# Routed tiles of a mixture-of-experts layer: turned in squares of 32 on VectorE instead of whole on TensorE

## The reference

```python
def _layernorm(x, axis=-1, eps=1e-05):
    m = jnp.mean(x, axis=axis, keepdims=True)
    v = jnp.var(x, axis=axis, keepdims=True)
    return (x - m) / jnp.sqrt(v + eps)

def _swiglu(x, w1, w2, w3):
    return jax.nn.silu(x @ w1) * (x @ w3) @ w2

# _L0_ffn_ref: D = 512, F = 352, E = 8, TOPK = 2
y = _swiglu(xf, sw1, sw2, sw3)                       # shared part
scores = jax.nn.softmax(xf @ gate_w, axis=-1)
weights, indices = jax.lax.top_k(scores, TOPK)
cw = jnp.zeros((N, E)).at[jnp.arange(N)[:, None], indices].add(weights)
for e in range(E):
    h = _swiglu(xf, rw1[e], rw2[e], rw3[e])
    y = y + cw[:, e:e + 1] * h

# reference
x = x + 0.5 * _L0_ffn_ref(_layernorm(x), ...)
x = x + _L0_attn_ref(_layernorm(x), ...)
x = x + 0.5 * _L0_ffn_ref(_layernorm(x), ...)
```

## Time and profile before

| | |
|---|---|
| runs | 1639.86 us median of 3 (1637.92 to 1640.12) |
| profiled execution | 1637.68 us, span 1635.9 us |
| PE busy | 1566.0 us, 96% of the span, 8356 instructions |
| DVE busy | 868.2 us, 53% |
| ACT busy | 657.3 us, 40% |
| POOL busy | 894.9 us, 55% |
| chain that ended last | PE 71%, DMA 9%, DVE 7% |
| tile stages, first to last write of a tile's output | 197.5 to 1579.3 us, the attention between them |

### The profile page before, as it was taken

The page is one execution under the profiler, slowest core; times in us unless marked ns, Lnnn a source line. Parts: engine busy times, 40 slices in busy tenths (PEclk is TensorE's granted clock), DMA queues, the critical chain, the costliest instruction groups (busy, mean ns, idle before and its releaser), DMA issues.

```text
span 1635.9 us, 24109 instructions
## 1 busy us (share of the span) xinstructions
PE 1566.0 (96%) x8356; PEld 1140.7 (70%) x8356; DVE 868.2 (53%) x1482; ACT 657.3 (40%) x974; POOL 894.9 (55%) x745
## 2 busy tenths in 40 slices
PE   6999999999998898999999999999999999999996
PEld 5777899999986674444444444337778898899985
DVE  4554322222267686777777777667554422222226
ACT  4421322232232315666666666763431222222321
POOL 3206385503756947787887878510405277333635
PEclk9999999999999999999999999999999999999998
DMA  9306454423363321212112121124105265333338
GB/s 338 136 1 229 180 187 168 152 78 133 119 214 121 84 66 45 40 30 45 34 36 44 31 36 23 25 51 134 58 1 187 93 232 183 127 132 133 133 91 256
DMA packets 89344, 180.15 MB, mean 110 GB/s; under 512 B 30224, under 2 KB 31120, under 8 KB 86928
## 3 DMA queue, kind: packets, MB, share of 16 engines
q1 hardware_dynamic: 76400, 104.95, 21.4%
q0 software_dynamic: 12832, 73.67, 12.7%
HBM read 106.48 MB, written 55.97 MB: 99 GB/s over the span
## 4 chain that ended last, share of the span: by engine, by line
PE 71%; DMA 9%; DVE 7%; ACT 3%; SPq 3%; issue 3%; POOL 3%; POOLq 0%; DVEq 0%; ACTq 0%
PE PS L1190 9%; PE PS L1192 9%; PE PS L1191 9%; PE PS L1423 7%; PE PS L1437 6%; PE PS L1404 6%; DMA xn<-x_routed 4%; PE PS L1453 3%; DMA xs<-x_routed 2%; PE PS L1327 2%; PE PS L1332 2%; PE PS L1330 2%; PE PS L1329 2%; PE PS L1331 2%; PE PS L1328 2%
## 5 line engine op out<-in xcount | busy, mean ns | idle before, releaser
L1676 ACT ACTIVATE PT<-PS 128x1024 f32<-128x1024 f32 x256 | 258.2, 1025 | 124.3 <-PE PS L1423 122.9
L1973 DVE TENSOR_REDUCE nmf_later<-PS 128x1 f32<-128x1024 f32 x160 | 194.1, 1219 | 58.2 <-PE PS L1404 57.7
L1437 PE MATMUL PS<-PT,V 128*32 128x512 f32 x1024 | 202.5, 604 | 0.0
L2041 POOL TENSOR_TENSOR W<-raw,W 128x544 fp32r<-128x544 f32 x144 | 190.0, 1353 | 1.5
L1423 PE MATMUL PS<-QS,KS 98*128 98x512 f32 x512 | 177.2, 430 | 3.7 <-DVE nmf_first L1973 2.0
L982 POOL TENSOR_TENSOR added<-PT 128x1024 f32<-128x1024 f32 x56 | 136.2, 2433 | 75.4 <-ACT PT L1676 75.4
L1423 PEld LDWEIGHTS PS<-QS,KS 98*128 98x128 f32 x512 | 84.8, 189 | 128.2 <-issue 50.7
L1404 PE MATMUL PS<-KS,QS 96*128 96x512 f32 x512 | 168.5, 411 | 5.1 <-ACT PT L1676 2.3
L1940 DVE TENSOR_TENSOR thid<-thid,PS 128x352 f32<-128x352 f32 x78 | 40.7, 521 | 245.7 <-ACT thid L1607 245.7
L2029 POOL DMA_DIRECT2D raw<-ffn_w x18 | 10.0, 554 | 248.6 <-POOLq L2027 192.3
L1190 PE MATMUL PS<-xh,W 128*128 128x512 f32 x352 | 141.7, 403 | 4.1 <-DVE xl L1703 1.6
(11 more groups left out here) (200 smaller groups left out, 3832.9 us busy)
## 6 DMA issues: line engine op xcount, KB each, us to landing
raw<-ffn_w POOLq DMA_DIRECT2D x18, 2176.0 KB, 10.4
y_routed<-ytile SPq DMA_DIRECT2D x78, 256.0 KB, 2.0
xn<-x_routed SPq DMA_DIRECT2D x40, 256.0 KB, 3.2
x_routed<-xq SPq DMA_DIRECT2D x1, 9984.0 KB, 29.4
xs<-x_routed SPq DMA_DIRECT2D x38, 256.0 KB, 3.8
QS<-later_hi SPq DMA_DIRECT2D x112, 64.0 KB, 2.0
raw<-ffn_w SPq DMA_DIRECT2D x6, 768.0 KB, 6.0
raw<-ffn_w SPq DMA_DIRECT2D x16, 272.0 KB, 4.2
```

Source lines behind the costliest of these rows:

```text
L1437: e.matmul(PS[i * QUARTER:(i + 1) * QUARTER, ob, :], V[:, b * QT + kt, g, :], PT[:, u % PTBUF, kt % 2 * GRP:(kt % 2 + 1) * GRP], start=rou ...
L1676: e.activation(PT[:, u % PTBUF, :], PS[:, i:i + 2, :].rearrange("p b n -> p (b n)"), ACT.Exp, scale=SCALE).then_inc(p_ready.sem, 1)
L1973: e.tensor_reduce(row_maxima(n)[:, h, t:t + 1], PS[:, i:i + 2, :].rearrange("p b n -> p (b n)"), AX.X, ALU.max, negate=True).then_inc(max_ ...
L2041: low = e.tensor_tensor(W[:, slot, 1, cs], raw[slot][:, cs], W[:, slot, 0, cs], ALU.subtract)
```

## The change

A tile is loaded by four DMAs of 32 partitions. Part q takes the features q * 128 to q * 128 + 127 of all 128 tokens: its partition i gets the four rows i, 32 + i, 64 + i and 96 + i, 128 features (512 bytes) of each. VectorE then turns every 32 x 32 square in place, over the whole 128 x 512 buffer in one instruction. After that partition 32 q + j holds, for square (a, c), the tokens 32 a to 32 a + 31 of the feature 128 q + 32 c + j. `xth` and `xtl` are made from that buffer in SBUF, through a view (`xcolumns`) that puts c outside. The rows of the experts' `w1` and `w3` are put in the matching order on the host (`square_rows`). TensorE's `turn_tile` is gone, with its four instructions for each tile, and so is the use of `BANK_G` for tiles. The load of tile i + 2 waits for `tile_lo` of tile i instead of `tile_turned`.

```diff
+SQ = 32
+    xcolumns = [of.rearrange("p (a c i) -> p c a i", a=P // SQ, i=SQ) for of in xtile]
-    tile_in = [signal(f"tile_in{i}", 16) for i in range(2)]
+    tile_in = [signal(f"tile_in{i}", 16 * P // SQ) for i in range(2)]
...
     def sync_program(e):
+        def tile_load(i):
+            for q in range(P // SQ):
+                e.dma_start(xtile[i % 2][q * SQ:(q + 1) * SQ, :].rearrange("i (a n) -> i a n", n=P),
+                            tile_rows(x_routed, i)[:, q * P:(q + 1) * P].rearrange("(a i) n -> i a n", i=SQ)
+                            ).then_inc(tile_in[i % 2].sem, 16)
...
-                e.dma_start(xtile[0], tile_rows(x_routed, 0)).then_inc(tile_in[0].sem, 16)
+                tile_load(0)
                 sp.wait_ge(a_done, s, last_first)
-                e.dma_start(xtile[1], tile_rows(x_routed, 1)).then_inc(tile_in[1].sem, 16)
+                tile_load(1)
...
                 if i + 2 < TILES:
-                    sp.wait_ge(tile_turned, s, i)
-                    e.dma_start(xtile[i % 2], tile_rows(x_routed, i + 2)).then_inc(tile_in[i % 2].sem, 16)
+                    sp.wait_ge(tile_lo, s, i)
+                    tile_load(i + 2)
...
     def tensor_program(e):
-        def turn_tile(s, i):
-            pe.wait_ge(tile_in[i % 2], s, i)
-            until_free(BANK_G)
-            for c in range(DC):
-                turned = e.transpose(PS[:, BANK_G, c * P:(c + 1) * P], xtile[i % 2][:, c * P:(c + 1) * P], identf[:])
-            turned.then_inc(tile_turned.sem, 1)
-            free[BANK_G] = (tile_lo, s, i)
...
-            if i + 1 < TILES:
-                turn_tile(s, i + 1)
...
     def scalar_program(e):
-            e.activation(xth[:], PS[:, BANK_G, :].rearrange("p (c n) -> p c n", c=DC), ACT.Copy).then_inc(tile_hi.sem, 1)
+            e.activation(xth[:].rearrange("p c (a i) -> p c a i", i=SQ), xcolumns[i % 2], ACT.Copy).then_inc(tile_hi.sem, 1)
...
     def vector_program(e):
+        def turn_tile(s, i):
+            dve.wait_ge(tile_in[i % 2], s, i)
+            e.transpose(xtile[i % 2], xtile[i % 2]).then_inc(tile_turned.sem, 1)
+
         def tile_columns_lo(s, i):
             dve.wait_ge(tile_hi, s, i)
-            e.tensor_tensor(xtl[:], PS[:, BANK_G, :].rearrange("p (c n) -> p c n", c=DC), xth[:],
-                            ALU.subtract).then_inc(tile_lo.sem, 1)
+            e.tensor_tensor(xtl[:].rearrange("p c (a i) -> p c a i", i=SQ), xcolumns[i % 2],
+                            xth[:].rearrange("p c (a i) -> p c a i", i=SQ), ALU.subtract).then_inc(tile_lo.sem, 1)
...
             elif kind == "tile_start":
+                turn_tile(*key, 0)
                 tile_columns_lo(*key, 0)
+                turn_tile(*key, 1)
             elif kind == "tile":
...
                 e.tensor_tensor(htl[:], PS[:, BANK_R, 0:FCH * P], hth[:], ALU.subtract).then_inc(thid_lo.sem, 1)
+                if i + 2 < TILES:
+                    turn_tile(s, i + 2)
...
+    def square_rows(w):
+        return w.reshape(P // SQ, DC, SQ, -1).transpose(1, 0, 2, 3).reshape(D, -1)
...
     def expert_unit(w1, w3, w2):
+        w1, w3 = square_rows(w1), square_rows(w3)
```

More of the change, by code:

```diff
@@ L812, in macaron @@
                 tile_in[i].plan(s, i)
-            for a in (tile_turned, tile_hi, tile_lo):
+            for a in (tile_hi, tile_lo):
                 a.plan(s, 0)
+            for i in range(2):
+                tile_turned.plan(s, i)
         elif kind == "tile":
@@ L823, in macaron @@
                 tile_in[i % 2].plan(s, i + 2)
+                tile_turned.plan(s, i + 2)
             if i:
@@ L1493, in tensor_program @@
                 tile_words(s)
-                turn_tile(s, 0)
             elif kind == "tile":
```

## The result

The change makes the kernel slower by 0.4%: 1643.66 us median (1636.68 to 1653.36, 20 runs) against 1637.95 us for the kernel before (1633.38 to 1641.21, 20 runs), a ratio of 1.004 with a 95% interval of 1.0028 to 1.0052. The forecast was 1623. The profiled execution took 1644.18 us, 1642.4 of them span. The 20 runs after fall into two groups of ten with medians of 1640.5 and 1648.5 us, where the same two groups of runs before lie at 1638.1 and 1637.8; what parts them is not shown, so the size of the loss is less sure than the interval says.

What follows compares the result with a forecast made beforehand. The prediction took TensorE, with no gap left in the tile stages, to bound the kernel. Turns spared, lock and loads summed as -33.4 + 12.7 + 6 = -14.7 us, from 1637.68 to 1623, range 1606 to 1640.

Steps and rivals of the forecast that it cites:

- The lock: `xtl`, now with two SBUF inputs, waits for the rest of one POOL instruction: +12.7 us, bounds 0 and 24.
- What TensorE is spared: Tile stages: each group of turns costs PE 0.44 us, items fall from 6.71 to 6.27, 76 groups save 33.4 us.
- What ACT and DVE do instead: Tile stages, undisturbed: `xth` 0.619 us, `xtl` 0.693, turn 0.69, all hidden, with 0.3 us of slack left before `xtl`.
- The deadline: A tile's load must land by 9.45 us after its issue, 0.24 earlier than before, or PE waits for `xtl`.
- The load: Ten tile loads behind weights land 0.4 us later against a deadline 0.24 earlier: +6 us, bounds 2 and 19.
- My upper bound: Tile loads behind weights, last issue's delay seen in full: 1.3 + 0.4 + 0.24 for each of ten, 19 us.
- the rival with turns packet by packet: DMA engines alternate between weights and tile queues; tiles land at 13.5 us, 31 us more, time 1648; chance 0.12.

Runs made afterwards that it cites:

- e1: The changed kernel with VectorE turning the squares into PSUM bank BANK_G, so `xtl` has one input in PSUM; ratio to before 0.99, that is 1622 us.
- e3: The changed kernel with both the turn into PSUM and a third tile buffer; ratio to before 0.9731, that is 1594 us.
- e2: The changed kernel with a third tile buffer, each load an item earlier, the turn still in SBUF; ratio to before 0.9887, that is 1619 us.
- e4: The kernel before the change, with only the third tile buffer added; ratio to before 0.9947, that is 1629 us.
- e7: The changed kernel with GpSimd waiting for its own step after each of eight casts, not once after the last; ratio to before 0.998, that is 1635 us.
- e6: The changed kernel with each tile loaded by four DMAs of whole 2 KB rows (feature order wrong); ratio to before 1.0046, that is 1645 us.

## Why the prediction was wrong

By the stages of the kernels above the four terms can be told apart. Loads are e1 less e3, less what they cost before (516.1 - 507.6 = 8.5). The lock is e2 less e3. What is left over of after less before is the last term. All come from one execution of each kernel. By the ratios they are -35, +19, +26 and -3, each of the first three uncertain by 6 to 9 us, as the intervals are.

| term | predicted, us | shown, us |
|---|---|---|
| PE spared its turns | -33.4 | -32.9 (e4, e3) |
| lock between DVE and POOL | +12.7 (0 to 24) | +24.9 (e2, e3) |
| loads later than before | +6 (2 to 19) | +20.9 (e1, e3, e4) |
| both at once, less than their sum | none | -5.6 |
| sum | -14.7 | +7.3 |

**What TensorE is spared** was right: items of 6.27 us, no gap from up to down products.

**What ACT and DVE do instead** was right too. `xth` took 0.63 for 0.62, the turn 0.70 for 0.69, `xtl` 0.69 where nothing meets it. In e3 PE waits for none of them. The turn was not always ahead of `thid`, though: behind a late load it holds `thid` back. In the example the tile landed 11.18 us after its first issue. The deadline that I had worked out for it, 9.45, is then passed by 1.73, and that with the 0.42 that the lock added to its `xtl` makes most of the 2.30 us lost, so the deadline itself held. It holds over the whole run too. In before twelve tiles pass their deadline of 9.69, by 8.7 us in all, and late loads cost 8.5 there (516.1 - 507.6).

**The lock** existed, and its step failed in size: "DVE waits for the rest of one POOL instruction". That holds for subtractions. Behind casts VectorE at times waits for the rest of the row, in after three times of 17 and up to 4.71 us of it, where the 0.07 us for a cast had assumed 0.59 at most. In e2, from which the 24.9 come, the `xtl` beyond 0.99 (0.69 and the 0.3 of slack) take 12.9 us beside subtractions, where the forecast had 11.7, and 7.5 beside casts, where it had 1.0; up to 3.4 more is the clock. e7 takes the waits for rows of casts away and gains 9 us. The Trainium skill, in "SBUF — State Buffer", section "Who interferes with whom", has the shared pair go to whoever issues first for the whole instruction, and the other blocked. The trace agrees that there is a lock. But the wait did not end with the instruction that held it, 5.61 us through eight casts of 0.59, and this `xtl` lost although its row starts 0.35 us before the first cast.

**The load**: the step that failed is "Behind weights the three later issues are covered by the weights themselves, so I take a landing 0.4 us later". The cover held, since the tile follows the end of the weights and not its last issue (the table under e6), but the 0.4 did not. With four issues the weights themselves came some 0.3 us later, and the tile 0.74 behind them instead of 0.18, so it was in after 11.2 us and not 10.3, 0.85 later in the median. My upper bound, with the last issue's delay seen in full, had 1.7 later. The count was off as well: ten late tiles at 1.5 us each would have been 15 us in all; in e1 thirteen pass the deadline of 9.45, by 23.1 us together, and in after fourteen by 24.3. With the clock, up to 8.5 us in e1, that covers the 29.4 of e1 less e3. The landing at 13.5 of the rival with turns packet by packet did not come: no part took over 11.34 from its own issue, and all but two tiles were in by 11.6 after their first issue. Its turns are there all the same, as the packets under e6 show; its sizes were wrong. I had given the weights 16 packets or so on each engine, and 128 packets over 16 engines are 8, as many as the tile of before has, so that both end together. And what is left of the tile then takes 0.7 us, not 3.3. The Trainium skill's rule that each engine goes round its queues packet by packet, in "DMA: Bandwidth & Descriptors", section "Queues, rings and completion order", is thus borne out by the trace (75 packets against 61), though I had read the 10.0 us against it.

**What was left out** is the clock. I had taken it as 1.00, as in the earlier trace rows. The two costs, small as most single stalls are, at times fell into one item or lasted several us, and PE then ran at 1.2 GHz for a while. That is up to 10 of the 39 us. In e1 the stages read 0.99 and 0.98, in e2 0.99 and 0.99, in e3 1.00: it comes with either kind of stall. Summed over stretches of 2 us through both stages, PE was at the lower level for 20.4 us in after, 17.0 in e1, 6.8 in e2, 10.2 in e7 and for none in before and e3, and at most half of each is lost. So of the loads' 20.9 up to 8.5 us is clock, of the lock's 24.9 up to 3.4, and of the 10.8 by which e7's stages are shorter than after's up to 5.1. I did not isolate it by an experiment of its own.

So the mechanisms were the ones forecast, the one gain was of the forecast's size, and the two costs stood at their upper bounds at the same time (24.9 for 24 and 20.9 for 19, well within their uncertainty), in part by the clock, which neither bound held. I had combined their middles: by the two upper bounds the sum would have been -33.4 + 24 + 19 = +9.6, 1647.

## What to carry to other kernels

A stage whose PE has no gap pays for each wait that is made in it, and at times twice, since the clock fell behind some of the stalls. Before moving work to VectorE, look for operations with two SBUF inputs beside rows of GpSimd instructions that are issued back to back, and give them an input in PSUM where a bank is free. When a transfer is split and goes out behind a large one, do not carry over its old landing time (here 0.85 us more), and load a buffer earlier. Here the same change with the turn written to PSUM and a third buffer is 2.7% faster than before instead of 0.4% slower.

## What the runs showed of the hardware that was not expected

- Eight casts of GpSimd, back to back, kept a two-input subtraction of VectorE from ending for 5.61 us, though in four other rows of casts one came in between two of them. With GpSimd waiting after each cast the longest was 1.80. Its own subtractions, back to back as well, let VectorE in after one. The lock costs GpSimd too: those took 1444 ns in the mean against 1353 before.
- The transpose of 128x512 in 32-bit squares takes 0.70 us in place in SBUF and 0.717 into PSUM (715 to 729 ns in all 78 of e1).
- A tile of 256 KB issued right behind 2176 KB of weights lands with the end of the weights, 0.16 to 0.18 us after them with one issue, 0.34 to 0.49 with four of 2 KB runs and 0.67 to 1.83 with four of 512 byte runs. Meanwhile the two queues start about as many packets as each other (75 and 61 in 4 us). With four issues the weights come in later too, at 10.8 and 11.2 us for 10.4 and 10.5.
- Stalls of PE of 1.6 to 4.4 us inside an otherwise full stage were followed by granted clocks of 0.73 to 0.81 over stretches of 7 to 9 us. The stages of e3, without such stalls, read 1.00. But stalls of the same size were not always followed by one: in e7 PE's matmuls stood idle for 2.16 and 0.56 us ahead of 1459.02 and 1460.13, and the clock read 1.00 from 1456 to 1464.
